# The first attention of a four-layer kernel: one projection per batch, operand rows stacked by DMA, separate banks for scores and exponents, and a later place for values and outputs

## The reference, cut to what matters

```python
xn = layernorm(x[b])                              # [128, 512]
q  = (Wq @ xn + bq) * keep                        # [64, 512], keep = mask > 0
k  = (Wk @ xn + bk) * keep
v  = Wv @ ctx[b] + bv
for each window w (128 columns) and head h (8 rows):
    s = q[h, w].T @ k[h, w] * 8 ** -0.5           # [128, 128], masked keys far below
    o[h, w] = softmax(s) @ v[h, w].T
x[b] = x[b] + mask[b] * (Wo @ gelu(o) + bo)
```

## Time and profile before

| | us |
|---|---|
| median of 3 runs | 1110.77 |
| lowest and highest run | 1109.35, 1111.75 |
| span of the profiled execution | 1113.1 |
| PE busy in the span | 956.4 (86%) |
| DVE busy | 710.9 (64%) |
| ACT busy | 459.4 (41%) |
| POOL busy | 368.4 (33%) |

### The profile page before, as it was taken

The page is one execution under the profiler, slowest core; times in us unless marked ns, Lnnn a source line. Parts: engine busy times, 40 slices in busy tenths (PEclk is TensorE's granted clock), DMA queues, the critical chain, the costliest instruction groups (busy, mean ns, idle before and its releaser), DMA issues. The chain is left out here.

```text
span 1113.1 us, 14911 instructions
## 1 busy us (share of the span) xinstructions
PE 956.4 (86%) x4939; PEld 617.6 (55%) x4939; DVE 710.9 (64%) x1186; ACT 459.4 (41%) x672; POOL 368.4 (33%) x352
## 2 busy tenths in 40 slices
PE   5888884999999999999887688899987698779997
PEld 2555552655666666664454344444464465447886
DVE  5676547396778777874958853477745788445434
ACT  2454432324656566662225332344412465334130
POOL 5244203104757656752221320200010122038431
PEclk9899865899999999999987799699997899979999
DMA  8000102233978967655404100000003100022001
GB/s 315 1 2 1 57 2 90 87 133 129 335 278 306 348 240 262 221 190 199 160 1 180 39 0 1 20 2 1 1 1 132 67 1 0 1 94 77 24 15 39
DMA packets 32988, 112.69 MB, mean 101 GB/s; under 512 B 4304, under 2 KB 4624, under 8 KB 29840
## 3 DMA queue, kind: packets, MB, share of 16 engines
q1 hardware_dynamic: 25392, 87.08, 21.3%
q0 software_dynamic: 7520, 24.65, 6.4%
HBM read 132.69 MB, written 16.78 MB: 134 GB/s over the span
## 5 line engine op out<-in xcount | busy, mean ns | idle before, releaser
L1208 POOL DMA_INDIRECT f_picks<-f_turn_xn,f_target x47 | 114.1, 2428 | 75.1 <-ACT f_turn_xn L1097 74.5
L1624 PE MATMUL banks<-f_t_dn,f_z 128*128 128x512 f32 x188 | 88.5, 593 | 0.6 <-issue 0.6
L1352 DVE TENSOR_TENSOR f_gu_lo<-f_t_gu,f_gu_hi 128x2048 fp32r<-128x2048 f32 x24 | 55.0, 2293 | 14.2 <-ACT f_gu_hi L1083 11.5
L1352 DVE TENSOR_TENSOR f_xn_lo<-f_t_gu,f_xn_hi 128x2048 fp32r<-128x2048 f32 x23 | 52.7, 2292 | 16.4 <-ACT f_xn_hi L1083 16.4
L1202 POOL DMA_INDIRECT f_turn_xn<-f_xn_rows,f_token x47 | 47.4, 1008 | 43.0 <-DVE f_token L1346 18.7
L106 POOL TENSOR_TENSOR a_ahead_var_eps<-mean_var,eps 128x1 f32<-128x1 f32 x16 | 3.0, 190 | 162.5 <-DVE mean_var L102 162.5
L2315 ACT ACTIVATE a_e<-banks 128x1024 f32<-128x1024 f32 x32 | 32.8, 1024 | 53.3 <-PE banks L2414 53.2
L1090 ACT ACTIVATE f_sil<-banks 128x256 f32<-128x256 f32 x47 | 18.1, 384 | 79.3 <-PE banks L255 79.3
L164 PE MATMUL banks<-ident,f_turn_xn 128*128 128x128 f32 x96 | 22.0, 384 | 32.6 <-DVE f_turn_xn L172 32.6
L1083 ACT CAST f_gu_hi<-f_t_gu 128x2048 fp32r x24 | 45.7, 1905 | 9.5 <-DMA f_t_gu<-in_f_gu 7.2
L1083 ACT CAST f_xn_hi<-f_t_gu 128x2048 fp32r x23 | 43.7, 1901 | 12.9 <-DMA f_t_gu<-in_f_gu 10.5
(11 more groups left out here) (415 smaller groups left out, 2635.5 us busy)
## 6 DMA issues: line engine op xcount, KB each, us to landing
f_t_gu<-in_f_gu SPq DMA_DIRECT2D x47, 1024.0 KB
f_t_dn<-in_f_dn SPq DMA_DIRECT2D x47, 512.0 KB, 4.4
f_t_gu<-f_picks SPq DMA_DIRECT2D x8, 1024.0 KB, 5.1
f_xn_rows<-f_turn_xn SPq DMA_DIRECT2D x9, 256.0 KB, 2.6
x_res<-in_x SPq DMA_DIRECT2D x8, 256.0 KB, 6.9
a_ctx<-in_ctx SPq DMA_DIRECT2D x2, 1024.0 KB, 13.5
a_out_mask<-in_mask SPq DMA_DIRECT2D x1, 2048.0 KB, 15.8
a_ct<-in_ctx_turned SPq DMA_DIRECT2D x4, 512.0 KB, 7.9
```

Of the source, the lines that this page charges most:

```text
L1208: pool.indirect_dma_start(dram["f0_picks_flat"], bass.IndirectOffsetOnAxis(ap=target[:, t:t + 1], axis=0), t_y[:, t % F0_BUFS, :], None).t ...
L1352: dve.tensor_tensor(t_gu_lo[t % 2], t_gu[:, bass.ds(i, 1), :, :].rearrange("p i c n -> p (i c n)"), t_gu_hi[t % 2].bitcast(F32), ALU.subtr ...
L1624: mm = pe.matmul(ps[:, TY_BANK + t % 2, :], t_zt[:, t % 2, c, :], t_dn[:, t % F0_BUFS, c, :], start=c == 0, stop=c == F0_IC - 1)
```

## The change: what it does

- One matmul per batch (`wqk`, 64 query rows and 64 key rows) in place of four. `keys_queries` on VectorE adds the bias and multiplies by the mask, `upper_part` on ScalarE rounds it, `lower_part` on GpSimd takes the rest (the first time on VectorE).
- The stacked operands are no longer computed. SyncE writes the parts to a DRAM tensor (`store`, five DMAs per batch) and reads them back stacked (`fetch`, four DMAs per batch) into `st`, one of three buffers. Constant rows are written once, by three DMAs. `x`, mask and `ctx` loads are spread between these.
- Three batches are projected before the units start. The order of `x` loads: 0 to 2 early, 3 behind `fetch(0)`, 4 and 5 behind `fetch(1)`, 6 and 7 behind `fetch(2)`. The statistics of batches 3 to 7 stand on VectorE ahead of the loop.
- Scores use banks 4 and 5, keyed scores banks 6 and 7. `scores(s)` waits for `maximum(s - 1)`, `keyed(s)` for `exponent(s - 1)`, and no longer for each other.
- `keyed(2u - 1)` runs in iteration u, `values(u - 1)` last in iteration u, `turn_outputs(u - 2)` and `divide(u - 2)` in iteration u. The bias of the values moves into gelu, whose argument it shifts equally. From batch 3 on, `normalise` is on GpSimd, and the mask takes one operation instead of two.

```diff
+A0_EARLY = 3
...
+            def batch_at(u):
+
+                return (u + 2 * A0_EARLY - 1) // 2 if u % 2 == 1 and u + 2 * A0_EARLY - 1 < 2 * B else None
+
+            def values_at(u):
+
+                return (u + 1) // 2 if u % 2 == 1 and (u + 1) // 2 < B else None
...
+                    def store(b):
+                        qs, ks = slice(0, A0_HEADS), slice(A0_HEADS, 2 * A0_HEADS)
+                        sp.wait_ge(qk_hi_ready, b + 1)
+                        hi, lo = qk_hi[:, b % 2, :].bitcast(F32), qk_lo[:, b % 2, :].bitcast(F32)
+                        sp.dma_start(part_of(b, slice(0, 2 * A0_HEADS), 0), hi).then_inc(parts_stored[b % 2], 16)
+                        sp.dma_start(part_of(b, qs, 1), hi[0:A0_DK]).then_inc(parts_stored[b % 2], 16)
+                        sp.dma_start(part_of(b, ks, 2), hi[A0_DK:P]).then_inc(parts_stored[b % 2], 16)
+                        sp.wait_ge(qk_lo_ready, b + 1)
+                        sp.dma_start(part_of(b, qs, 2), lo[0:A0_DK]).then_inc(parts_stored[b % 2], 16)
+                        sp.dma_start(part_of(b, ks, 1), lo[A0_DK:P]).then_inc(parts_stored[b % 2], 16)
+
+                    def fetch(b):
+                        sp.wait_ge(parts_stored[b % 2], 16 * A0_WRITES * (b // 2 + 1))
+                        if b < A0_BUFS:
+                            sp.wait_ge(st_zeroed, b + 1)
+                        else:
+                            sp.wait_ge(keyed_done, 2 * A0_GROUPS * (b - A0_BUFS + 1))
+                        for r in range(A0_PER_GROUP):
+                            sp.dma_start(st[r * A0_SLOT:r * A0_SLOT + A0_ROWS, b % A0_BUFS, :, :].bitcast(F32),
+                                         parts[b, r::A0_PER_GROUP].rearrange("j e n -> e j n")).then_inc(st_loaded[b % A0_BUFS][r // 2], 16)
...
+                    store(0)
+                    sp.wait_ge(fixed_stored, 16 * 3)
+                    fetch(0)
+                    load_x(3)
+                    store(1)
+                    fetch(1)
+                    load_x(4)
+                    load_x(5)
+                    store(2)
+                    fetch(2)
+                    load_x(6)
+                    load_x(7)
...
+                    load_ctx(2)
+                    load_ctx(3)
+                    fetch(3)
...
+                    for b in range(4, B):
+                        store(b)
+                        fetch(b)
...
+                    def normalise(b):
+                        pool.wait_ge(first.rstd_ready, b + 1)
+                        pool.wait_ge(proj_done, b - 1)
...
+                    lower_part(1)
+                    clear(1)
+                    kept(2)
+                    lower_part(2)
...
+                    clear(2)
+                    for b in range(3, B):
                         first.scale(pool, b)
...
+                        kept(b)
+                        normalise(b)
+                        lower_part(b)
...
+                    def upper_part(b):
+                        act.wait_ge(qk_ready, b + 1)
+                        if b >= 2:
+                            act.wait_ge(parts_stored[b % 2], 16 * A0_WRITES * (b // 2))
+                        act.copy(qk_hi[:, b % 2, :], qk[:, b % 2, :]).then_inc(qk_hi_ready, 1)
...
+                    for b in range(A0_EARLY):
+                        upper_part(b)
+                    take_values(0)
                     for u in range(UNITS + 1):
+                        if u >= 1:
+                            exponent(2 * u - 1)
+                        if batch_at(u) is not None:
+                            upper_part(batch_at(u))
+                        if values_at(u) is not None:
+                            take_values(values_at(u))
                         if u < UNITS:
                             exponent(2 * u)
-                            exponent(2 * u + 1)
                         if u >= 1:
                             take_out(u - 1)
-                        if u == 0:
-                            split_q(2)
-                        if u + 2 < UNITS:
-                            split_k(u + 2)
-                        if u + 3 < UNITS:
-                            split_q(u + 3)
...
+                    def keys_queries(b):
...
+                            dve.wait_ge(qk_lo_ready, b - 1)
+                        dve.scalar_tensor_tensor(out=qk[:, b % 2, :], in0=ps[:, QK_BANK, :],
+                                                 scalar=cols[:, C_B:C_B + 1], in1=keep_of(b), op0=ALU.add,
+                                                 op1=ALU.mult).then_inc(qk_ready, 1)
...
                     def maximum(s):
                         dve.wait_ge(scores_done, s + 1)
+                        if s >= 2:
+                            dve.wait_ge(max_turned, s // 2)
                         dve.tensor_reduce(
                             mx[:, :, PAIR * (s % 2) + A0_MAX_ROW:PAIR * (s % 2 + 1):A0_SLOT].rearrange(
                                 "p w r -> p r w"),
-                            ps[:, s_banks(s), :].rearrange("p r (w j) -> p r w j", w=A0_WINS),
+                            ps[:, S_BANK:S_BANK + 2, :].rearrange("p r (w j) -> p r w j", w=A0_WINS),
                             AX.X, ALU.max, negate=True).then_inc(max_ready, 1)
...
                     def lower(u):
                         dve.wait_ge(max_turned, u + 1)
-                        dve.wait_ge(q_ready, u + 1)
-                        dve.tensor_tensor(q[:, u % 2, :], ps[:, M_BANK, :], q[:, u % 2, :].bitcast(F32), ALU.add)\
+                        if u >= 2:
+                            dve.wait_ge(keyed_done, 2 * u - 2)
+                        dve.tensor_tensor(qm[:, u % 2, :], ps[:, M_BANK, :],
...
                     dve.wait_ge(cols_ready, 1)
-                    dve.wait_ge(first_mask_loaded, 16)
-                    key_mask(dve, 0, first_mask_ready, 0)
+                    dve.wait_ge(mask_loaded[0], 16)
+                    keep(dve, 0).then_inc(first_keep_ready, 1)
+                    keys_queries(0)
                     statistics(1)
                     statistics(2)
-                    stack(0)
-                    stack(1)
+                    dve.wait_ge(qk_hi_ready, 1)
+                    dve.tensor_tensor(qk_lo[:, 0, :], qk[:, 0, :], qk_hi[:, 0, :].bitcast(F32),
+                                      ALU.subtract).then_inc(qk_lo_ready, 1)
                     normalise(1)
-                    statistics(3)
-                    statistics(4)
+                    keys_queries(1)
+                    normalise(2)
+                    keys_queries(2)
+                    dve.wait_ge(mx_zeroed, 1)
                     maximum(0)
                     maximum(1)
-                    statistics(5)
-                    values_biased(0)
-                    for u in range(UNITS + 1):
+                    for b in range(A0_EARLY, B):
+                        statistics(b)
+                    for u in range(UNITS + 2):
+                        if u + 1 < UNITS:
+                            maximum(2 * u + 2)
+                        if batch_at(u) is not None:
+                            keys_queries(batch_at(u))
+                        if u >= 2:
+                            divide(u - 2)
                         if u < UNITS:
                             lower(u)
-                        if u == 0:
-                            statistics(6)
-                            statistics(7)
-                        if u + 2 < UNITS:
-                            stack(u + 2)
-                        if u % 2 == 1 and (u + 1) // 2 < B:
-                            values_biased((u + 1) // 2)
-                        if u % 2 == 0 and u // 2 + 2 < B:
-                            normalise(u // 2 + 2)
                         if u + 1 < UNITS:
-                            maximum(2 * u + 2)
                             maximum(2 * u + 3)
-                        if u >= 1:
-                            divide(u - 1)
                     dve.wait_ge(out_mask_loaded, 16)
                     for b in range(B):
...
+                    def project(b):
...
+                        pe.matmul(ps[:, QK_BANK, :], wqk, xn[:, b % 2, :], start=True, stop=True).then_inc(proj_done, 1)
...
 
                     def scores(s):
...
+                        b = u // A0_GROUPS
+                        pe.wait_ge(st_loaded[b % A0_BUFS][s % 2], 16 * 2 * (b // A0_BUFS + 1))
+                        if s >= 1:
+                            pe.wait_ge(max_ready, s)
+                        for rows, r, w, win in heads(pair(s), A0_ROWS):
+                            mm = pe.matmul(ps[:, S_BANK + r % 2, win], q_of(u, rows, win), k_of(u, rows, win),
...
                     def keyed(s):
                         u = s // 2
...
+                        if s >= 1:
+                            pe.wait_ge(exp_ready, s)
+                        for rows, r, w, win in heads(pair(s), A0_ROWS):
```

(47 more changed lines are left out.)

310 lines of the change are left out of this document (130 added, 180 removed).

## The result

The changed kernel took 1127.96 us (median of 4 runs, 1123.90 to 1133.61), the kernel before 1111.26 beside it (1109.35 to 1113.86): a ratio of 1.0135, 95% interval 1.0102 to 1.0168. It is slower by 1.35%, clear of the noise. Forecast were 1095 and at most 1113. The profiled execution of the changed kernel took 1124.89 us.

The account below looks back on a forecast made before the run. It took the first attention's units as bound by a ring of waits with TensorE nearly filled. Start +14.2, with the steps -15.1 at the last `lower`, and end -1 made -16: 1095 us, range 1078 to 1113 (forecast's own 1087 to 1102).

Parts of the forecast that it names:

- The start: Ahead of the first attention's units: `lower(0)` on VectorE comes at 37.3 instead of 23.13, 14.2 us lost.
- the steps: Fifteen unit steps of the first attention: 4.97 or 5.93 us at full clock, 93 us in all with half clock.
- the end: From the last `lower` to the last `divide` of the first attention: 9.7 us instead of 10.7.
- landing 2.3: In each store and fetch turn through DRAM at the start: a DMA lands 2.3 us after its issue.
- rival B: DMA round trips nearer 5 us than 2.3, three trips and a load adding 11 us: 1106 us; chance 0.15.
- 16 keyed matmuls 0.62 (96.10 to 96.72), so 8 take 0.31: TensorE's issue time for one keyed half in each step, taken as half of the 16 matmuls' time.
- 40% half clock: Share of the units' time at half clock, the largest unknown, giving a mean step of 6.2 us.
- The clock: In the units, gaps on TensorE bring the throttled clock back; half-clock steps take 8.4 us against 5.3.
- The 27% before: Share of the units' time at half clock in the kernel before: 32 us of 122.
- Rival C: The clock stays at half in the units: 1129 us, or 1118 at a share of 0.85; chance 0.13.
- No wait for `st` in the loop: In the unit loop, `scores` never waits for the DMA into `st`.
- the start's own bound: Bounds on the start's loss: +17 with landings of 6.9 us, -1 with landings of 2.0.

Follow-up runs that it names:

- e1: Changed kernel with the loads of x 3 to 7 issued up front behind x 2: 1114.25 us, ratio 1.0029 to the kernel before.
- e2: Changed kernel with the statistics of batches 4 to 7 moved into VectorE's loop: 1114.03 us, ratio 1.0023 to the kernel before.
- e3: Changed kernel without the three constant-row DMAs, fetches taking 24 rows instead of 26: 1122.76 us, ratio 1.0121 to the kernel before.
- e7: e4 plus two unused 256-column matmuls in every even step of TensorE's loop: 1100.24 us, ratio 0.9892 to the kernel before.
- g1: Changed kernel plus two unused 256-column matmuls per even step: 1119.01 us, ratio 0.9998 to the kernel before, with widely spread runs.
- h1: g3 run again in more rounds beside h2: 1098.83 us, ratio 0.9886 to the kernel before.
- g4: g3 without the fills of the last steps and the output stage: 1099.73 us, ratio 0.9876 to the kernel before.
- h3: g3 with store 1 issued ahead of fetch 0 and store 2 ahead of fetch 1: 1094.16 us, ratio 0.9843 to the kernel before.
- g3: Changed kernel, mask load behind x 1, x 3 to 7 between stores and fetches, statistics in the loop, fill matmuls everywhere: 1098.29 us, ratio 0.9839.
- h2: Kernel before with fill matmuls ahead of its loop, in every step and in the output stage: 1098.80 us, ratio 0.9873 to the kernel before.
- e4: Changed kernel with the edits of e1 and e2 together: 1111.85 us, ratio 1.0024 to the kernel before.
- g2: Kernel before with one unused 256-column matmul per step, 16 in all: 1103.35 us, ratio 0.9937 to the kernel before.

## Why the prediction was wrong

By its own sum the forecast was -16, and the span became 10.0 longer, 26 us apart. The start made 17.8 of it, the steps 10.3, the end and the output stage 0.8, and the rest of the kernel gave back 2.8.

- **The start, +14.2 foretold, +32.0 measured.** The place was right (`lower(0)` behind the statistics of `x` 7), e1 and e2 show it; the size was not. The failed term is "landing 2.3". It came from single writes of 256 KB, and with a turn's traffic it was 4.3, 5.1 and 5.8; the last loads of `x` took 6.0 instead of 3. Together some 11 us, which is what rival B had: its term was right, and its price. The other 6.5 us are issues: the last store of batch 0 was issued by 17.75 instead of 11.9, since issues of 2.95, 4.16 and up to 1.65 us stood where 0.48 was put, which e3 traces to the constant rows. No rival had that term. Fetch 0, put from 14.2 to 16.1, came from 22.0 to 23.6.
- **The steps, 93 foretold, 103.3 measured.** At full clock they are 5.26 and about 6.27 instead of 4.97 and 5.93, 5.60 instead of 5.3. The failed number is "16 keyed matmuls 0.62 (96.10 to 96.72), so 8 take 0.31": 8 took 0.59 (106.22 to 106.81); `turn_max` took 0.59 (107.82 to 108.41) where 0.44 was put, and smaller terms came out shorter. At 40% half clock, 5.60 gives 1 / (0.6 / 5.60 + 0.4 / 8.4) = 6.46, 96.9 us: 3.9 of the 10.3. The half-clock share of 49% instead of 40% gives 1 / (0.51 / 5.60 + 0.49 / 8.4) = 6.69, 100.4 us: another 3.5. The last 2.9 are that a step at half the clock cost more than 8.4, by this sum 9.1; the granted 0.50 stood in the steps with a projection and not in those of 5.26.
- **The clock.** That idle time of TensorE brings it down in the loop was right and is shown by e7 and g1; that it isn't the whole of it, by h1. The 27% before were read from the granted clock alone: with the half speed from 23.1 to about 28, which the record doesn't show, it was some 30%. Rival C, half clock nearly throughout, did not come. That its 1129 lies beside the measured 1127.96 is luck.
- **The end**, 9.7: 158.41 to the last `divide` at 168.4 took 9.95. Right.
- **No wait for `st` in the loop**: right for the changed kernel; one of 3.2 us stood ahead of it. g4 and h3 had one within it, of 0.2 and 1.0.
- **The range.** The start's own bound, +17 more with landings of 6.9, was nearly what came (17.8), and alone would have ended at 1112 or 1113, just inside. The steps had no bound for their full-clock price, and the range left out both going wrong together.

So the account is: at full clock the steps would gain 15 x (7.23 - 5.60) = 24 us by the estimate above. With fills in both kernels they gained 10.1 (h1), 17.0 (g3) and 19.7 (h3) against h2's 111.7, since part of them ran at half the clock, and the start gave 15.4, 15.4 and 17.8 back (37.7, 37.7 and 40.1 against 22.3), even where it is mended. The next layer started 4.7 us later than in h2 in h1, and 2.2 and 2.6 earlier in g3 and h3. That is why a change that takes three of four projections away is worth next to nothing here.

What stays open: why some 4 us pass for a store to DRAM with half the fetch in flight, what keeps the clock at 0.50 while TensorE is busy throughout, whether the change is faster than the kernel before at really the same clock, and what h3 would gain over h1 and h2 in more runs.

## What to carry to other kernels

Price a round trip through DRAM from a row with the same traffic beside it, and ask which unrelated load has been queued behind its wait and which engine's queue stands behind that load. When work is taken off TensorE, look at the granted clock before and after: compare both kernels with the same fill in TensorE's idle time, and read the granted clock of both again, or the clock is taken for the change. Where the record shows 1.00, check it against the duration of a matmul that is known at full clock. Don't halve a group of small matmuls by their count; see first how many row slots they fill at once.

## What the runs showed of the hardware that was not expected

- Matmuls in different row slots run side by side: 8 in two slots took 0.59 us to the next group, 16 in four slots 0.62; the interleaved 8 scores and 8 `keyed` of the other slots took 0.61 (108.41 to 109.02).
- Three writes with constants, read from 8 partitions, made later DMA issues last 2.95 and 4.16 us instead of 0.43 (changed kernel against e3).
- The recorded clock can be 1.00 while matmuls take twice their time: a projection's matmul 2.07 us at 59.9 instead of 1.02 (changed kernel).
- More matmuls made the kernel faster: 16 fills gave 11.6 us (e7 against e4), the granted clock 0.97 instead of 0.75 from 79.9 to 136.6; on the kernel before 16 gave 0.6% (g2).
